# GpSimd as a third issuer for the last tile's stores and loads in a DLRM tower

## The chip, the cores and the metric

The kernel runs on one NeuronCore of a Trainium2 chip. A core has TensorE (matrix products, results in PSUM), VectorE, ScalarE, GpSimd and SyncE (SP), and its transfers run on 16 DMA engines. Transfers are issued by SP, ScalarE or GpSimd, each with a queue of its own. The metric is the device time of one execution in microseconds; a kernel's time is the median of its runs.

## What is computed

2048 samples have 26 indices each and a dense vector of 128 numbers. The 26 table rows (128 numbers each) and the dense vector make 27 vectors per sample. All 351 dot products of two different ones of them, with the dense vector appended, go through three layers (479 to 512 to 256 to 1), all in float32:

```
e = stack([tbl_f[ids[:, f]] for f in range(26)], axis=1)      # 2048 x 26 x 128
T = concatenate([r_dense[:, None, :], e], axis=1)             # 27 vectors a sample
Z = einsum('bnd,bmd->bnm', T, T)
h = concatenate([Z[:, iu0, iu1], r_dense], axis=1)            # pairs n < m, then dense
h = maximum(h @ W_top1 + b_top1, 0.0)
h = maximum(h @ W_top2 + b_top2, 0.0)
y = h @ W_top3
```

## The kernel before

The samples are cut into 16 tiles of 128. Two tiles make a unit; there are 8 units, and `END` is 7, the last. For each tile, GpSimd gathers the rows of 16 tables from DRAM by indirect transfers (L418), 16 to a tile; the rows of the ten small tables are looked up on TensorE as products with one-hot columns (`look`). TensorE turns the gathered rows (`turn`), ScalarE copies what was turned or looked up into `T`, and TensorE makes all dot products of a tile in four blocks (`products`, L773), into `gram_ps`. VectorE copies each block into `gram` (L488, semaphore `gram_free`).

In `gram`, the dot products lie by vector in the partitions. For the first layer they must lie by pair in the partitions and by sample along the row. So they go out to DRAM and come back. Four stores (`dots_store`, j = 0 to 3) take 27 partitions of `gram` each. For a unit (two tiles) they go to `dots`, in pieces of 64 numbers (256 B). Then the loads (`pairs_load`, chunks c = 0, 1, 2 of up to 117 pairs each, and `far_load`, 13 rows that belong to chunk 2) bring them back into `pairs`.

The last unit's two tiles are not stored together but one by one, l = 0 and l = 1, to `dots_last`, in pieces of 32 numbers (128 B): 27 x 27 = 729 pieces to a store, 91 KB. SP does this for l = 0 (L345 to L356). For l = 1 there is nothing left in the loop to work on, and the work is spread over two queues: SP issues the stores j = 0, 1 and later the loads of chunks 0 and 2, ScalarE the stores j = 2, 3 (`last_store`, L644) and later the load of chunk 1 and the far rows (`last_load`, L649 and L650). Each issuer waits for all four stores, which together raise `dots_last_stored[1]` to `STORED`, 64, before it issues a load; every transfer adds 16 when it has landed.

TensorE then does the first layer of tile l = 1 (`last_layer1`, L814): first the dense part for the four groups f of 128 outputs, then chunk by chunk:

```
for c in range(PC):
    for f in range(F1C):
        mm = product(f, c, PC)
        if c == PC - 1:
            mm.then_inc(l1_done, 1)
```

`product` waits for the chunk's semaphore `shuffled_last[1][c]`, 16, or 32 for chunk 2, whose far rows are a second load. After it come ScalarE's activations (L636), the second layer (L836), and VectorE's last sums (L507, L509), whose result SP sends out (L392).

GpSimd has no work after its last gather, that of tile 15. Each engine's instructions run in the order in which they are written; between engines only semaphores set the order.

Of the kernel before, what the change touches and what calls it, by code (L numbers as in the profile page):

```python
# [18 lines left out]
BLOCKS = 4  # L19
# [44 lines left out]
def dlrm_tower(nc, r_dense, ids, tables, W1, b1, W2, b2, W3, out):  # L64
# [6 lines left out]
    TILES = B // P  # L71
# [34 lines left out]
    with ExitStack() as ctx:  # L106
# [6 lines left out]
        def sem(name):  # L113
            return ctx.enter_context(nc.semaphore(name))
# [53 lines left out]
        shuffled = [sem(f"shuffled{i}") for i in range(2)]  # L168
        dots_last_stored = [sem(f"dots_last_stored{l}") for l in range(2)]
        shuffled_last = [[sem(f"shuffled_last{l}_{c}") for c in range(PC)] for l in range(2)]  # L170
        stored = sem("stored")
        ident_zero = sem("ident_zero")
        ident_ready = sem("ident_ready")
# [125 lines left out]
        def _(sp):  # L299
# [45 lines left out]
            def shuffle_last(l, groups, chunks):  # L345

                sp.wait_ge(gram_free, BLOCKS * (2 * END + l + 1))
                for j in groups:
                    sp.dma_start(*dots_store(dots_last[l], j, l * NI, (l + 1) * NI)).then_inc(dots_last_stored[l], 16)
                if l == 0:  # L350
                    sp.wait_ge(l1_done, 2 * (END - 1))
                sp.wait_ge(dots_last_stored[l], STORED)
                for c in chunks:
                    sp.dma_start(*pairs_load(dots_last[l], c, last_pairs(l, c))).then_inc(shuffled_last[l][c], 16)
                if l == 0:
                    sp.dma_start(*far_load(dots_last[l], last_pairs(l, PC - 1))).then_inc(shuffled_last[l][PC - 1], 16)  # L356
# [30 lines left out]
                    load_pair_weights(1)  # L387
                    sp.dma_start(w2[:], W2.rearrange("(c p) f -> p c f", p=P)).then_inc(weights_landed, 16)
            shuffle_last(0, range(NJ), range(PC))
            shuffle_last(1, range(NJ // 2), range(0, PC, 2))  # L390
            sp.wait_ge(y_ready, 2 * UNITS)
            sp.dma_start(out.rearrange("(p t) o -> p (t o)", p=P), y[:]).then_inc(stored, 16)  # L392
            sp.wait_ge(stored, 16)
# [1 line left out]
        @block.gpsimd  # L395
        def _(pool):
            nc.gpsimd.memset(ident[:], 0.0).then_inc(ident_zero, 1)
            pool.wait_ge(ident_zero, 1)
            nc.gpsimd.affine_select(out=ident[:], in_=ident[:], compare_op=ALU.not_equal, fill=1.0, base=0,
                                    pattern=[[-1, P]], channel_multiplier=1).then_inc(ident_ready, 1)  # L400
            nc.gpsimd.iota(minus_row[:], pattern=[[0, 1]], base=0, channel_multiplier=-CH,
                           allow_small_or_imprecise_dtypes=True).then_inc(minus_row_ready, 1)

            def gather(t):
                if t == 0:
                    pool.wait_ge(ids_first_landed, 16)
                if t == 1:
                    pool.wait_ge(ids_landed, 16)
                index = ids_first if t == 0 else ids_all[:, t]
                for r in range(NR):  # L410
                    if t >= 2:
                        pool.wait_ge(turned, NR * (t - 2) + r + 1)
                    if t == 1 and r == 2:
                        pool.wait_ge(ids_rows_stored, 16)
                    for n in rounds[r]:
                        if n == 0:
                            continue
                        pool.indirect_dma_start(  # L418
                            rows[:, t % 2, place[n], :], None, tables[n - 1],
                            bass.IndirectOffsetOnAxis(ap=index[:, n - 1:n].bitcast(U32), axis=0),  # L420
                        ).then_inc(rows_landed[t % 2][r], 16)

            for t in range(TILES):
                gather(t)

        @block.vector
        def _(dve):
# [150 lines left out]
        def _(act):  # L578
# [61 lines left out]
            def last_store(groups):  # L640

                act.wait_ge(gram_free, BLOCKS * TILES)
                for j in groups:
                    act.dma_start(*dots_store(dots_last[1], j, NI, 2 * NI)).then_inc(dots_last_stored[1], 16)  # L644

            def last_load(chunks):
                act.wait_ge(dots_last_stored[1], STORED)
                for c in chunks:
                    act.dma_start(*pairs_load(dots_last[1], c, last_pairs(1, c))).then_inc(shuffled_last[1][c], 16)  # L649
                act.dma_start(*far_load(dots_last[1], last_pairs(1, PC - 1))).then_inc(shuffled_last[1][PC - 1], 16)  # L650
# [62 lines left out]
            turn_out(END, 1, 3)  # L713
            h1_out(END - 1, 1)
            turn_out(END, 1, 4)
            last_store(range(NJ // 2, NJ))
            last_h1_out(0)
            last_load(range(1, PC, 2))
            last_h1_out(1)

        @block.tensor
        def _(pe):
# [84 lines left out]
            def last_layer1(l):  # L807
                def product(f, c, first):
                    if c == PC:
                        rhs, kk = dense[:, END % 2, l * P:(l + 1) * P], P  # L810
                    else:
                        pe.wait_ge(shuffled_last[l][c], 32 if c == PC - 1 else 16)
                        rhs, kk = pairs[:KP, END % 2, c, l * P:(l + 1) * P], KP
                    return pe.matmul(last_l1(l, f), w1[:kk, c, f * P:(f + 1) * P], rhs,  # L814
                                     start=(c == first), stop=(c == PC - 1))
# [127 lines left out]
```

## Time and profile before

| what | value |
|---|---|
| median of 3 runs | 367.7 us (367.35 to 368.36) |
| the profiled execution's own time | 367.51 us |
| its span, from the first to the last instruction | 365.7 us |
| TensorE busy | 343.7 us, 94% |
| VectorE, ScalarE, GpSimd busy | 223.3, 172.5, 255.7 us |
| mean granted TensorE clock | 0.985 of full speed |

The span is measured on one profiled execution; 1.8 us of its time lie outside it. A TensorE busy for 94% leaves little waiting, and a share over the whole span says nothing on a single place: the rows below are those of the places that the change touches. Times in rows count from the span's start.

### The profile page before, as it was taken

To read this page: it belongs to the slowest core of one execution; us is meant where nothing else is said; L and a number is where in the kernel's file an instruction comes from. 1 tells how busy PE (TensorE), PEld (TensorE's weight loads), DVE (VectorE), ACT (ScalarE), POOL (GpSimd) and SP (SyncE) were. 2 spreads that over 40 slices of the span, in tenths; PEclk is the share of its full clock that TensorE was granted. 3 is DMA by queue.
4 is the path that set the end of the run, shared out by engine and by line. 5 is a ranking of instruction groups with operands and counts; after the bars stand their busy time and mean duration, and the time that the engine had idled before them with its cause. 6 is when DMAs were issued, how large, how long until landed. Compare 5 with 4: busy or idle time off the path is not lost.

```text
span 365.7 us, 9897 instructions
## 1 busy us (share of the span) xinstructions
PE 343.7 (94%) x4042; PEld 321.2 (88%) x4042; DVE 223.3 (61%) x786; ACT 172.5 (47%) x220; POOL 255.7 (70%) x263
## 2 busy tenths in 40 slices
PE   3997898879899999999999999999999999999976
PEld 1887798869889999999989998999999998998866
DVE  3989969976826485556927394656828493622311
ACT  4266737553456244553466153643476154435111
POOL 6788877777777777777777777777777777775000
PEclk9999999989999999999999999999999999999986
DMA  7996232353525522354225522462225321544030
GB/s 206 262 257 189 66 124 62 92 144 109 179 59 135 170 58 52 87 130 147 58 52 138 167 60 50 103 182 79 60 52 136 96 60 52 120 112 86 21 61 1
DMA packets 45878, 39.07 MB, mean 107 GB/s; under 512 B 32930, under 2 KB 39113, under 8 KB 45834
## 3 DMA queue, kind: packets, MB, share of 16 engines
q1 hardware_dynamic: 36014, 21.40, 22.1%
q0 software_dynamic: 8192, 16.79, 17.4%
q8 instruction: 32, 0.52, 0.6%
q10 hardware_dynamic: 1628, 0.25, 0.5%
q14 instruction: 12, 0.10, 0.1%
HBM read 32.40 MB, written 6.02 MB: 105 GB/s over the span
## 4 chain that ended last, share of the span: by engine, by line
PE 82%; DMA 6%; ACT 6%; DVE 3%; issue 2%; ACTq 0%; SPq 0%; DVEq 0%
PE look_ps L747 35%; PE gram_ps L773 15%; PE mlp_ps L793 13%; PE look_ps L757 7%; PE mlp_ps L803 7%; DMA ids_near<-ids_rows 2%; ACT T L614 2%; PE look_ps L738 2%; DVE hot L464 2%; DMA ids_rows<-rows 1%; DMA dots_last<-gram 1%; ACT T L606 1%; ACT tab_hi L582 1%; PE mlp_ps L814 1%; DMA ids_all<-in_ids_dram 1%
## 5 line engine op out<-in xcount | busy, mean ns | idle before, releaser
L418 POOL DMA_INDIRECT rows<-in_tbl_dram,ids_all x240 | 236.9, 987 | 73.2 <-issue 71.3
L464 DVE TENSOR_SCALAR hot<-ids_near 125x256 fp32r<-125x256 f16 x640 | 149.1, 304 | 41.9 <-PE look_ps L747 35.4
L747 PE MATMUL look_ps<-hot,tab_hi 125*128 125x256 f32 x616 | 154.4, 290 | 6.4 <-DVE tab_lo L447 2.2
L747 PE MATMUL look_ps<-hot,tab_lo 125*128 125x256 f32 x616 | 150.2, 283 | 0.0
L747 PEld LDWEIGHTS look_ps<-hot,tab_hi 125*128 125x128 f32 x616 | 117.8, 191 | 8.2 <-issue 3.8
L747 PEld LDWEIGHTS look_ps<-hot,tab_lo 125*128 125x128 f32 x616 | 118.1, 192 | 0.1
L614 ACT COPY T<-look_ps 128x384 f32<-128x384 f32 (+1 forms) x80 | 85.3, 1109 | 69.1 <-PE look_ps L757 69.0
L488 DVE COPY gram<-gram_ps 128x432 f32<-128x432 f32 x64 | 38.8, 607 | 68.6 <-PE gram_ps L773 66.5
L606 ACT COPY T<-look_ps 128x512 f32<-128x512 f32 x32 | 38.7, 1208 | 74.2 <-PE look_ps L747 69.0
L773 PEld LDWEIGHTS gram_ps<-T 128*54 128x54 f32 x2048 | 54.5, 131 | 8.2 <-issue 4.5
L773 PE MATMUL gram_ps<-T 128*54 128x54 f32 x2048 | 57.8, 215 | 1.9 <-DVE gram L488 1.2
L757 PE MATMUL look_ps<-ident,rows 128*128 128x128 f32 x272 | 41.8, 277 | 1.2 <-issue 1.2
L793 PE MATMUL mlp_ps<-pairs,w 117*128 117x256 f32 x168 | 40.9, 379 | 0.0
L757 PEld LDWEIGHTS look_ps<-ident,rows 128*128 128x128 f32 x272 | 31.3, 142 | 3.3 <-issue 1.4
L793 PEld LDWEIGHTS mlp_ps<-pairs,w 117*128 117x128 f32 x168 | 30.7, 189 | 3.7
L803 PE MATMUL mlp_ps<-w,h 128*128 128x256 f32 x112 | 25.4, 380 | 0.9 <-ACT h L629 0.9
L803 PEld LDWEIGHTS mlp_ps<-w,h 128*128 128x128 f32 x112 | 20.7, 190 | 3.7 <-ACT h L629 1.1
L629 ACT ACTIVATE h<-mlp_ps,bias 128x128 f32<-128x128 f32 x56 | 16.1, 383 | 12.9 <-PE mlp_ps L793 12.9
L418 POOL DMA_INDIRECT rows<-in_tbl_dram,ids_first x16 | 18.0, 1124 | 5.7 <-issue 4.6
L591 ACT ACTIVATE ids_near<-ids_near,minus_row 125x2560 f16<-125x2560 f16 x7 | 17.1, 2441 | 0.7 <-DMA ids_near<-ids_rows 0.7
L793 PE MATMUL mlp_ps<-dense,w 128*128 128x256 f32 x56 | 16.7, 379 | 0.0
L602 ACT COPY T<-look_ps 128x256 f32<-128x256 f32 x16 | 11.3, 706 | 6.4 <-PE look_ps L747 6.0
(72 smaller groups left out, 137.3 us busy)
## 6 DMA issues: line engine op xcount, KB each, us to landing
dots<-gram SPq DMA_DIRECT2D x28, 182.2 KB
ids_near<-ids_rows SPq DMA_DIRECT2D x7, 640.0 KB, 6.2
rows<-in_tbl_dram,ids_all POOLq DMA_INDIRECT x240, 2.6
T<-in_tbl_dram SPq DMA_DIRECT2D x5, 448.0 KB
pairs<-dots SPq DMA_DIRECT2D x14, 117.0 KB
rows<-in_r_dense_dram SPq DMA_DIRECT2D x16, 64.0 KB
gram<-in_tbl_dram SPq DMA_DIRECT2D x2, 448.0 KB
pairs<-dots SPq DMA_DIRECT2D x7, 104.0 KB
```

What stands on the lines that cost most here:

```text
L418: pool.indirect_dma_start(rows[:, t % 2, place[n], :], None, tables[n - 1], bass.IndirectOffsetOnAxis(ap=index[:, n - 1:n].bitcast(U32), a ...
L464: eq = nc.vector.tensor_scalar(hot[:VP, at % 2, c], ids_near[:VP, u % 2, k], float(c), None, ALU.is_equal)
L488: nc.vector.tensor_copy(gram[:, :, :, first:first + PER], gram_ps[:, b % 2, 0:2 * PER * NV].rearrange("p (i s n) -> p s n i", s=2, n=NV)). ...
L591: nc.scalar.activation(ids_near[:VP, u % 2], ids_near[:VP, u % 2], ACT.Identity, bias=minus_row[:VP]).then_inc(ids_relative, K)
L606: nc.scalar.copy(T_unit(u)[:, :, :, n0:n1 + 1:n1 - n0].rearrange("p l q n -> p n l q"), src.rearrange("p (n l q) -> p n l q", n=2, l=2)).t ...
L614: nc.scalar.copy(T_tile(u, l)[:, :, n:n + cnt].rearrange("p q n -> p n q"), look_ps[:, bank_of(("turn", u, l, r)), 0:cnt * P].rearrange("p ...
L629: relu = nc.scalar.activation(by_sample[:, g], by_pair[:, g], ACT.Relu, bias=bias1[:, f:f + 1])
L747: mm = pe.matmul(dst, w[:VP, k, c], hot[:VP, slot, c], start=(c == 0 and half == 0), stop=(c == CH - 1 and half == 1))
L757: mm = pe.transpose(look_ps[:, bank, i * P:(i + 1) * P], rows[:, l, place[n], :], ident[:])
L773: mm = pe.matmul(gram_ps[64 * g:64 * g + 2 * NV, b % 2, at:at + 2 * NV], src[:, g, i], src[:, g, i], start=True, stop=True)
L793: mm = pe.matmul(mlp_ps[:, f * 2 // F1C, f % 2], w1[:kk, c, f * P:(f + 1) * P], rhs, start=(c == 0), stop=(c == PC))
L803: mm = pe.matmul(mlp_ps[:, 0, l], h1[:, c, l * P:(l + 1) * P], w2[:, c], start=(c == 0), stop=(c == F1C - 1))
```

## The change

For the last tile, l = 1, GpSimd becomes a third issuer. It sends store j = 3, which ScalarE sent, once the last copy is done, and loads chunk 2, which SP loaded. It gets two semaphores, `pool_stored` for its store and `pool_loaded` for its load. SP keeps stores 0, 1 and chunk 0; ScalarE keeps store 2, chunk 1 and the far rows. All three wait for `pool_stored` at 16 and `dots_last_stored[1]` at 48 before they load. TensorE waits, before chunk 2, for `pool_loaded` and for the far rows. Nothing else is changed; the transfers are the same eight, in the same sizes.

```diff
+        pool_stored = sem("pool_stored")
+        pool_loaded = sem("pool_loaded")
...
                 if l == 0:
                     sp.wait_ge(l1_done, 2 * (END - 1))
-                sp.wait_ge(dots_last_stored[l], STORED)
+                if l == 0:
+                    sp.wait_ge(dots_last_stored[l], STORED)
+                else:
+                    sp.wait_ge(pool_stored, 16)
+                    sp.wait_ge(dots_last_stored[l], STORED - 16)
...
             shuffle_last(0, range(NJ), range(PC))
-            shuffle_last(1, range(NJ // 2), range(0, PC, 2))
+            shuffle_last(1, range(NJ // 2), range(1))
...
             for t in range(TILES):
                 gather(t)
+
+            pool.wait_ge(gram_free, BLOCKS * TILES)
+            pool.dma_start(*dots_store(dots_last[1], NJ - 1, NI, 2 * NI)).then_inc(pool_stored, 16)
+            pool.wait_ge(pool_stored, 16)
+            pool.wait_ge(dots_last_stored[1], STORED - 16)
+            pool.dma_start(*pairs_load(dots_last[1], PC - 1, last_pairs(1, PC - 1))).then_inc(pool_loaded, 16)
...
             def last_load(chunks):
-                act.wait_ge(dots_last_stored[1], STORED)
+                act.wait_ge(pool_stored, 16)
+                act.wait_ge(dots_last_stored[1], STORED - 16)
...
-            last_store(range(NJ // 2, NJ))
+            last_store(range(NJ // 2, NJ - 1))
             last_h1_out(0)
-            last_load(range(1, PC, 2))
+            last_load(range(1, PC - 1))
             last_h1_out(1)
...
-                        pe.wait_ge(shuffled_last[l][c], 32 if c == PC - 1 else 16)
+                        if l == 1 and c == PC - 1:
+                            pe.wait_ge(pool_loaded, 16)
+                        pe.wait_ge(shuffled_last[l][c], 32 if l == 0 and c == PC - 1 else 16)
```

The end of SP's queue before, from the far rows of tile l = 0 on; a row is a line of the kernel, the transfer, what it writes and reads, its shape and its waits:

```order
L356 DMA pairs<-dots_last 13x128
L349 DMA dots_last<-gram 729x1x32 [waits gram_free]
L349 DMA dots_last<-gram 729x1x32
L354 DMA pairs<-dots_last 117x1x128 [waits dots_last_stored1]
L354 DMA pairs<-dots_last 104x1x128
L392 DMA out_dram<-y 128x16 [waits y_ready]
```

And now (lines of the changed kernel are counted anew):

```order
L362 DMA pairs<-dots_last 13x128
L351 DMA dots_last<-gram 729x1x32 [waits gram_free]
L351 DMA dots_last<-gram 729x1x32
L360 DMA pairs<-dots_last 117x1x128 [waits dots_last_stored1,pool_stored]
L398 DMA out_dram<-y 128x16 [waits y_ready]
```

The load of 104 rows, chunk 2, has left the queue, and the load of chunk 0 waits for one more semaphore.

The end of ScalarE's queue before, with the activations of both tiles' first layer (L636) around its loads:

```order
L644 DMA dots_last<-gram 729x1x32 [waits gram_free]
L644 DMA dots_last<-gram 729x1x32
L636 ACTIVATE h<-look_ps,bias 128x2x2x32 [waits l1_done]
L636 ACTIVATE h<-look_ps,bias 128x2x2x32
L636 ACTIVATE h<-look_ps,bias 128x2x2x32 [waits l1_done]
L636 ACTIVATE h<-look_ps,bias 128x2x2x32
L649 DMA pairs<-dots_last 117x1x128 [waits dots_last_stored1]
L650 DMA pairs<-dots_last 13x128
```

And now:

```order
L656 DMA dots_last<-gram 729x1x32 [waits gram_free]
L648 ACTIVATE h<-look_ps,bias 128x2x2x32 [waits l1_done]
L648 ACTIVATE h<-look_ps,bias 128x2x2x32
L648 ACTIVATE h<-look_ps,bias 128x2x2x32 [waits l1_done]
L648 ACTIVATE h<-look_ps,bias 128x2x2x32
L662 DMA pairs<-dots_last 117x1x128 [waits dots_last_stored1,pool_stored]
L663 DMA pairs<-dots_last 13x128
```

One store is gone from ahead of the activations. It stands now at the end of GpSimd's queue, behind the gathers of tile 15, with the load of chunk 2 behind it:

```order
L424 DMA rows<-in_tbl_dram,ids_all 128x128 [waits turned]
L424 DMA rows<-in_tbl_dram,ids_all 128x128
L433 DMA dots_last<-gram 729x1x32 [waits gram_free]
L436 DMA pairs<-dots_last 104x1x128 [waits dots_last_stored1,pool_stored]
L106 UNCONDITIONAL_BRANCH
```

Before, the branch that ends the queue followed the gathers.

## Rows read from the trace of the kernel before

**Rows 1.** The page: shares of the engines in the chain that ended last.

```profile
PE 82%; DMA 6%; ACT 6%; DVE 3%; issue 2%; ACTq 0%; SPq 0%; DVEq 0%
```

**Rows 2.** The chain of work, last 20 us: start us, us, what.

```profile
346.11 0.62 DVE gram L488
...
346.75 1.62 ACTq L644
...
348.41 4.11 DMA dots_last<-gram
352.51 0.02 issue
352.53 2.51 DMA pairs<-dots_last
...
355.08 1.22 PE mlp_ps L814 x4
...
358.87 0.85 PE mlp_ps L814 x4
```

**Rows 3.** Timeline, 346 to 354, ScalarE and SP: start us, us, engine, line.

```profile
346.74 1.58 SPq L349 DMA_DIRECT2D dots_last<-gram  x2
...
346.75 2.44 ACTq L644 DMA_DIRECT2D dots_last<-gram  x2
349.23 1.27 ACT L636 ACTIVATE h<-look_ps,bias 128x128 f32<-128x128 f32 x4 [9.61 <-issue]
```

**Rows 4.** Windows of 0.25 us (last two columns: DMA share, GB/s); packets, 347 to 352.4.

```profile
348.00:348.25 0.25, 0.25 (x5) 0.25 (x4) 0.23 (x2) 0.00 (x0) 0.00 (x0) 1.00 0.14 27
...
349.25:349.50 0.25, 0.25 (x5) 0.25 (x4) 0.00 (x0) 0.25 (x2) 0.00 (x0) 1.00 0.77 122
...
351.25:351.50 0.25, 0.25 (x3) 0.20 (x3) 0.00 (x0) 0.00 (x0) 0.00 (x0) 1.00 0.91 96
351.50:351.75 0.25, 0.25 (x4) 0.25 (x3) 0.06 (x1) 0.00 (x0) 0.00 (x0) 1.00 0.50 51
...
DMA packets 2952, 0.37 MB, mean 69 GB/s; under 512 B 2952, under 2 KB 2952, under 8 KB 2952
```

**Rows 5.** DMA view, 314.3 to 321.9, a unit's stores: share in 40 slices, queues.

```profile
DMA  0746566677437478976656987683697766349300
...
q1 hardware_dynamic: 2952, 0.75, 44.4%
```

**Rows 6.** TensorE's last dense products; windows with its clock (third from last); L814 alone.

```profile
351.94 0.61 PE L814 MATMUL gram_ps<-dense,w 128*128 128x128 f32 x4
...
354.50:354.75 0.25, 0.00 (x0) 0.00 (x0) 0.00 (x0) 0.00 (x0) 0.00 (x0) 0.69 0.52 156
354.75:361.25 6.50, 6.17 (x27) 5.99 (x28) 0.00 (x0) 1.50 (x4) 0.00 (x0) 0.50 0.05 14
...
346.20:349.60 3.40, 3.40 (x32) 3.40 (x31) 1.00 0.30 50
355.40:360.50 5.10, 5.10 (x24) 4.88 (x23) 0.50 0.01 2
```

**Rows 7.** GpSimd's gathers: timeline, windows and the page's list of issues.

```profile
329.38 0.94 POOL L418 DMA_INDIRECT rows<-in_tbl_dram,ids_all  x1 [0.30 <-issue]
...
334.39 0.95 POOL L418 DMA_INDIRECT rows<-in_tbl_dram,ids_all  x1 [0.30 <-issue]
...
330.25:331.00 0.75, 0.75 (x5) 0.67 (x4) 0.72 (x2) 0.75 (x1) 0.44 (x2) 1.00 0.00 0
331.00:331.25 0.25, 0.25 (x3) 0.22 (x2) 0.25 (x3) 0.15 (x1) 0.25 (x1) 1.00 0.84 197
...
rows<-in_tbl_dram,ids_all POOLq DMA_INDIRECT x240, 2.6
```

**Rows 8.** Another fall of the clock: timeline of TensorE, windows.

```profile
76.66 0.36 PE L747 MATMUL look_ps<-hot,tab_hi 125*128 125x256 f32 x1 [2.17 <-DVE tab_lo L447]
...
78.25:81.25 3.00, 2.84 (x34) 2.47 (x35) 2.06 (x10) 1.57 (x2) 2.36 (x3) 0.50 0.33 88
```

## The prediction

> **What bounds the kernel now.** I read the page's own list of the costliest chain first: TensorE carries it nearly to the end, so what matters is where TensorE stands still [rows 1]. Then I read the chain of work over the last 20 us in order of time [rows 2]. It shows one hole. The last copy of the products ends at 346.11 + 0.62 = 346.73. From there the chain is ScalarE's queue issuing (1.62 us), a store in flight (4.11 us), a load in flight (2.51 us), and only at 355.08 does TensorE go on; from 355.08 to the end it is TensorE, then VectorE, then the output. The change touches the stretch from 346.73 to 355.08, and nothing ahead of it.
>
> In that stretch both queues start at once, SP at 346.74 and ScalarE at 346.75, and each issues two stores [rows 3]. The windows by DMA share show the first data at about 348.2, some 100 to 120 GB/s until 351.50, and a window about half full after that [rows 4]. So the four stores divide into 1.45 us before any data, 351.63 - 348.2 = 3.4 us of data, and 352.51 - 351.63 = 0.88 us from the last data to the release of the loads (351.63 is where I put the end in the half-full row 351.50:351.75). The data do not wait for the issues: the last issue begins at 348.41 [rows 2] and ends at 346.75 + 2.44 = 349.19 [rows 3], over two microseconds before the last data.
>
> What holds the data back? The packets of the stretch are 2952, which is 4 x 738, and a store has 729 pieces of 128 B [rows 4]; 738 is 729 + 9, so I read nine engines per store with one closing packet each. Four stores one tile earlier in the loop, with pieces of 256 B, are 2952 packets too, but those spread over some 6.8 us instead of 3.4, 36 of the 40 slices of 0.19 us [rows 5], with gathers beside them. Twice the bytes, twice the time: the limit lies in the DMA engines that carry the pieces, and not in issuing. One store is worth 3.4 / 4 = 0.85 us of that.
>
> **The change, part by part.**
>
> *ScalarE's second store goes.* ScalarE is free at 346.75 + 1.62 = 348.37 instead of 349.19, 0.82 us earlier; its activations began at 349.23, right behind the issue [rows 3]. They make TensorE's following products ready sooner by a few tenths. Worth nothing at the end, since after those and the dense products TensorE stands idle from 352.55 for 2.5 us anyway [rows 2, 6]. The three hardware stores, alone, would have their last data at 351.63 - 0.85 = 350.78 and be landed at 350.78 + 0.88 = 351.66. That is the most that this part gives: 0.85 us.
>
> *GpSimd's store comes in.* GpSimd's last gather starts at 334.39 and takes 0.95 us [rows 7], so the engine has been idle for 11 us when the copies end and can start at about 346.8. Its issue is the unknown price, call it G. The trace has no plain GpSimd transfer, only gathers of 128 rows of 512 B. From below, G is what a gather takes, 0.95 us, if the number of pieces costs nothing. From above, all of the 0.95 us is work per row: 7.4 ns a piece, times 729, 5.4 us. I take the middle, 3.2 us, because some of a gather's time must be fixed and nothing in the rows says how much. After the issue a gather's data show 0.68 us later (issue 329.38 + 0.94 = 330.32, data in the window from 331.00, and none in the one before) [rows 7]. Then the store's own data, at most 0.85 us, and 0.88 us to land. Sum: 346.8 + G + 0.68 + 0.85 + 0.88 = 349.21 + G. With G = 0.95 that is 350.2, below the hardware stores' 351.66, so those decide and the gain is 0.85. With G = 3.2 it is 352.4, next to no gain. With G = 5.4 it is 354.6, a loss of 2.1 us. Data that start before the issue ends, or more engines than nine, would pull the middle down by some tenths; for these I take about half of the 0.85, so the middle lands at 352.0.
>
> *Shared engines.* If the GpSimd store sits on the same nine engines as the others, the 2952 packets stay on them and only an earlier start could help. By the Trainium skill (DMA: Bandwidth & Descriptors, Why a DMA increments its semaphore by 16 and not by 1), a transfer runs on the largest count up to 16 that divides the outer size of both sides, for hardware queues the lowest engines; the trace agrees, with 9 closing packets for 27 partitions against 729 rows. For GpSimd it names consecutive engines from a moving start; no row here shows which.
>
> *The waits.* SP, ScalarE and GpSimd wait for two semaphores where they waited for one; both are full before they go, or the later decides. Queued behind that wait on SP is the load of chunk 0, for which TensorE waits at 355.08; on ScalarE it is chunk 1 and, behind it, the last layer's activations, which are not due before the last chunk's products, from 358.87 on [rows 2].
>
> *Chunk 2 goes from SP to GpSimd.* TensorE takes the chunks in turn: the stretch of the chain from 355.08 to 358.87 covers chunks 0 and 1 [rows 2]. So chunk 2 is wanted 3.8 us after chunk 0, even at twice the clock 1.9 us after. A gather of slightly more data needs 2.6 us from issue to landing [rows 7], chunk 0 needs 2.51: chunk 2 lands about when chunk 0 does. Nothing, with 3 us of cover. SP's queue loses an issue that nobody waited for.
>
> *The clock.* TensorE's granted clock falls from full to half (2.4 to 1.2 GHz) at about 354.6, two microseconds into its idle time (from 351.94 + 0.61 = 352.55), and is still half until 361.25 [rows 6]. So nearly all of the last layer runs at half clock. The same kind of products takes 5.1 us for 24 there and 3.4 us for 32 at full clock [rows 6], 212 ns against 106 each. I keep that state in the sum.
>
> **The sum.** Landing of the stores, 352.51, becomes about 352.0, and all that follows moves by 0.5: 367.51 (the profiled execution's own time) - 0.5 = 367.0. The median of the runs shown is 0.2 above that execution, so 367.2.
>
> **The rivals.**
>
> *No gain, because the engines were the limit.* The third queue brings the same 738 packets to the same engines; landing stays at 352.5 and the time at 367.7. For it: the level rate across the seam between the queues, and the 256 B stores. Against it: whatever of the load goes to the seven others. The Trainium skill has this as a rule (DMA: Bandwidth & Descriptors, Issuing engines are not separate DMA queues): transfers from several issuers interleave on the same 16 engines, and more issuers only save issue time. By it the gain is nil here.
>
> *Slower, because GpSimd writes the pieces one by one.* Place: GpSimd's issue of the store, between 346.8 and the loads. It decides from G = 3.3 us on, 4.5 ns a piece, and is over the measurement's 1.1 us (0.3%) from G = 4.4. At the gather's full 7.4 ns a piece the time is 367.7 + 2.1 = 369.8. For it: this transfer has nearly six times as many pieces as a gather. Against it: a gather must look up an index for each row, a plain store needn't. A gentler case, G from 3.3 to 4.4, is no change.
>
> *Clearly faster, because the clock holds.* If TensorE waits 1.7 us instead of 2.5, it goes on at 354.2, ahead of the 354.6 where the clock fell. If the clock then stays full, the 6.5 us at half clock [rows 6] become some 3.2 us: 367.7 - 0.8 - 3.2 = 363.7. For it: the fall comes late in the idle time. Against it: at 78 us the clock falls while TensorE is busy, over a microsecond after a shorter idle stretch of 2.17 us [rows 8]; a fall is not ended by work that has just begun.
>
> **How the numbers follow.** A measurement of this kernel can tell about 1.1 us (0.3%). Small gain, 0.2 to 0.8 us: 0.40. No gain through shared engines or G of 3 to 4.4: 0.24. Slower through G above 4.4: 0.26. Clock holds: 0.10. The first two are "same" but for a little at the edges: faster 0.13, same 0.60, slower 0.27. The range goes up to 369.8, the price of 7.4 ns a piece, and down to 366.3, which is the full 0.85 us and the runs' own scatter of 0.6; only the clock's case and a dearer GpSimd than the bound lie outside.
>
> **What would show it.** GpSimd's queue has a transfer on the products at about 346.8, and its length is G. Right: the loads are released between 351.7 and 352.4, by a hardware store, and TensorE goes on 2.5 us later. Wrong towards slower: GpSimd's issue runs past 350, SP's loads wait for it, and the data share falls to nothing before the GpSimd packets come. Shared engines: the data end at 351.5 again. The clock's case: no half clock in the last ten microseconds. Chunk 2 would be wrong if TensorE had a wait between its second and third chunk.

## The result and the profile after

The changed kernel takes 369.37 us (median of 22 runs) against 366.28 us for the kernel before (22 runs); the ratio of the times is 1.008, 95% interval 1.0059 to 1.0101, some 3 us slower by the medians. One of the changed kernel's 22 runs took 560.11 us at a mean clock of 0.566; it is left out of the ratio. The profiled execution took 369.87 us, its span is 368.1 us, its mean granted clock 0.985.

The chain of work of the changed kernel, its last 20 us (start us, us, what), answers to [rows 2]:

```profile
347.66 0.62 DVE gram L500
...
349.13 5.84 DMA dots_last<-gram
...
355.03 2.45 DMA pairs<-dots_last
...
357.52 1.22 PE mlp_ps L829 x4
358.74 0.85 PE gram_ps L829 x4
...
366.12 0.06 DVEq L106
```

Times here must be counted from the end of the last copy, 347.66 + 0.62 = 348.28. From there to the loads, 355.03, it is 6.75 us; before it was 352.53 - 346.73 = 5.80 us. I call this the **stretch**, and it grew by 0.95. The store that ends it comes from SP's queue, a hardware one, and is 5.84 us in flight; before, the one at the chain's end was 4.11. Behind the stretch nothing changed: load 2.45 us, and from TensorE's first chunk to the last row's end 366.18 - 357.52 = 8.66 us at half clock. The rest of the difference between the two spans, 348.28 - 346.73 = 1.55 us, stands ahead of the copies, where nothing was changed; I come back to it.

The timeline of the changed kernel, 346 to 358, answers to [rows 3] (in brackets: us that the engine sat idle before, and what ended it):

```profile
348.30 1.60 SPq L351 DMA_DIRECT2D dots_last<-gram  x2
348.30 1.62 ACTq L656 DMA_DIRECT2D dots_last<-gram  x1
...
348.57 1.01 POOL L433 DMA_DIRECT2D dots_last<-gram  x1 [12.15 <-DVE gram L500]
...
349.97 0.64 ACT L648 ACTIVATE h<-look_ps,bias 128x128 f32<-128x128 f32 x2 [8.79 <-PE look_ps L829]
...
355.58 0.63 POOL L436 DMA_DIRECT2D pairs<-dots_last  x1 [6.00 <-DMA dots_last<-gram]
...
357.52 0.80 PE L829 MATMUL mlp_ps<-pairs,w 117*128 117x128 f32 x2 [3.52 <-DMA pairs<-dots_last]
```

GpSimd's issue of 729 pieces took 1.01 us, no longer than a gather of 128 rows [rows 7]. It was done at 349.58. ScalarE's only store took it 1.62 us, as the first of two did before, and SP's two took 1.60 together. So all issues were over by 349.92, five microseconds before the release, and issuing isn't what made it late. TensorE's wait went from 2.5 to 3.52 us, and it had no other wait between chunks.

The DMA view of the changed kernel, 347 to 356 (the last number of an issue is us to landing; a queue's last number is the time of its packets as a share of the 16 engines' time):

```profile
DMA packets 2279, 0.39 MB, mean 44 GB/s; under 512 B 2251, under 2 KB 2251, under 8 KB 2278
...
q1 hardware_dynamic: 1476, 0.19, 13.7%
q0 software_dynamic: 64, 0.10, 9.8%
q10 hardware_dynamic: 738, 0.09, 7.0%
...
dots_last<-gram POOLq DMA_DIRECT2D x1, 91.1 KB, 5.1
```

And the same view of the kernel before, 345 to 354:

```profile
q10 hardware_dynamic: 1476, 0.19, 16.1%
q1 hardware_dynamic: 1476, 0.19, 13.7%
```

A store that the hardware queues send is 738 packets. GpSimd's is 64 at most, 27 of them between 2 and 8 KB (2278 - 2251): its 729 pieces travel some 27 to a packet. Its packets took 9.8% of the engines' time, ScalarE's store of the same bytes 7.0% here and 16.1 / 2 = 8.05% before. But the three queues add up to 13.7 + 9.8 + 7.0 = 30.5%, and the two of before to 29.8%, so the packets' time hardly grew; and it isn't a measure of the engines' work, since a window below shows a share of 1.15, which only packets that overlap in time can give. And GpSimd's store landed at 348.57 + 5.1 = 353.7, 1.3 us before the loads were released. It was neither the last nor the quick one.

Windows of 0.25 us of the changed kernel (last two columns: DMA share, GB/s), with the clock third from last; they answer to [rows 4] and [rows 6]:

```profile
350.50:350.75 0.25, 0.25 (x4) 0.25 (x4) 0.00 (x0) 0.11 (x1) 0.00 (x0) 1.00 1.15 113
...
351.25:351.50 0.25, 0.25 (x4) 0.22 (x3) 0.00 (x0) 0.08 (x1) 0.00 (x0) 1.00 0.56 37
...
353.50:353.75 0.25, 0.25 (x5) 0.25 (x3) 0.21 (x2) 0.00 (x0) 0.00 (x0) 1.00 0.43 52
353.75:354.00 0.25, 0.25 (x3) 0.06 (x1) 0.25 (x2) 0.00 (x0) 0.00 (x0) 1.00 0.13 17
...
357.00:363.50 6.50, 5.98 (x26) 5.89 (x27) 0.00 (x0) 1.50 (x4) 0.00 (x0) 0.50 0.06 19
```

Data went until about 353.9, 5.6 us after the copies; before it was 351.63 - 346.73 = 4.9 us, and they ended within one window. The level rate of before is gone: in the midst of the data it falls to 37 GB/s for a window, and at the end it thins out from 353.5 on, over half a microsecond. Half a microsecond in the midst of it by queue, 351.0 to 351.5, 2.7 us after the copies:

```profile
q0 software_dynamic: 15, 0.02, 56.2%
q10 hardware_dynamic: 42, 0.01, 6.5%
q1 hardware_dynamic: 20, 0.00, 3.2%
```

and of the kernel before at the same distance, 349.5 to 350.0:

```profile
q10 hardware_dynamic: 358, 0.04, 57.7%
q1 hardware_dynamic: 124, 0.02, 20.1%
```

The two hardware queues moved 62 packets where they moved 482. While GpSimd's packets are under way the hardware stores nearly stand still: by half microseconds from 350.0 they move 308, 233, 62, 170 and 323 packets. The profiles of e1, e5, e12, e16 and e18 have the same gap, with 48 to 66 packets in the half microsecond at that distance.

The clock is at half (1.2 GHz) from 357.00 to beyond 363.50, about as long as in the profile of before.

### The profile page after: what moved, and what is told of

It reads as the page before. It is cut to its first block, busy times and chain, and to the rows that moved or that the text cites. A ratio compares the mean times of both kernels' runs of the same rounds, so it can differ in the third digit from the quotient of the medians.

```text
span 368.1 us, 9904 instructions
## 1 busy us (share of the span) xinstructions
PE 343.4 (93%) x4042; PEld 320.9 (87%) x4042; DVE 222.9 (61%) x786; ACT 172.3 (47%) x220; POOL 258.3 (70%) x265
## 4 chain that ended last, share of the span: by engine, by line
PE 81%; DMA 6%; ACT 6%; DVE 3%; issue 2%; SPq 0%; DVEq 0%; ACTq 0%
PE look_ps L760 35%; PE gram_ps L786 15%; PE mlp_ps L806 13%; PE look_ps L770 7%; PE mlp_ps L816 7%; DMA ids_rows<-rows 2%; ACT T L626 2%; DMA dots_last<-gram 2%; PE look_ps L751 1%; DVE hot L476 1%; DMA ids_near<-ids_rows 1%; ACT T L618 1%; ACT tab_hi L594 1%; PE mlp_ps L829 1%; DMA ids_all<-in_ids_dram 1%
## 5 line engine op out<-in xcount | busy, mean ns | idle before, releaser
L641 ACT ACTIVATE h<-mlp_ps,bias 128x128 f32<-128x128 f32 x56 | 16.1, 383 | 12.9 <-PE mlp_ps L806 12.9
```

The source lines that it names most:

```text
L641: relu = nc.scalar.activation(by_sample[:, g], by_pair[:, g], ACT.Relu, bias=bias1[:, f:f + 1])
```

## The experiments

Experiments e1 to e11 ran on chips on which every kernel, the one before too, took 505 to 540 us, with TensorE standing still in the loop (busy for 75 to 77% of the span in e1 to e4 and e8, against 94%). Their whole times decide nothing: e2 and e8, whose stretch is that of before and for which a ratio within 0.002 of 1 was expected, have 0.9951 and 0.9935, while e3 and e4, with the stretch longer and shorter, both have 1.0049. Only durations of the last stretch are read from them. e12 to e18 ran on chips where the kernel before takes 366 to 367.5 us.

**Store alone (e1, e16) and load alone (e2, e15).** One half of the change each:

```diff
-            shuffle_last(1, range(NJ // 2), range(1))
+            shuffle_last(1, range(NJ // 2), range(0, PC, 2))
...
-            pool.dma_start(*pairs_load(dots_last[1], PC - 1, last_pairs(1, PC - 1))).then_inc(pool_loaded, 16)
```

(e1, against the changed kernel; e2 has the load and leaves all four stores as before.)

> Only the store goes to GpSimd, chunk 2 stays with SP. In the profile of the changed kernel the stretch from the last copy to the release of the loads is 6.69 us against 5.78 before. Theory A (GpSimd's pieces hold up the hardware stores' data): the stretch stays at 6.5 to 6.9 us here, and the whole time is as far above the kernel before as the changed kernel, ratio 1.006 to 1.010. Rival B (the load on GpSimd costs something, at the end or elsewhere): the ratio falls to 1.002 or less although the stretch is long, and the rest of the loss belongs to the load.

> Only the load of chunk 2 goes to GpSimd; both stores stay with ScalarE. Theory A: the stretch from the last copy to the release of the loads is 5.8 us as before, the load lands under the products of chunks 0 and 1, ratio 1.000 within 0.002. Rival B: ratio 1.003 or more, with TensorE waiting ahead of its third chunk or losing time elsewhere.

> Only the store j = 3 is GpSimd's. Late theory: stretch 6.5 to 7 us, and the changed kernel's whole loss, 2 to 3 us, ratio 1.005 to 1.009. Early theory: the same loss or less, with the hole at 93 us over 2 us.

> Only the load of chunk 2 is GpSimd's; the four stores stay with SP and ScalarE. Late theory (the loss is the longer stretch of the stores and the clock that falls in it): as before, ratio 0.998 to 1.002, stretch 5.8 us. Early theory (something that any addition to GpSimd's queue brings, seen as TensorE's hole at 93 us, 2.35 to 3.6 us long in three profiles with the change and 0.8 to 1.2 us in two without): hole over 2 us, and the time 1 to 2 us above before, ratio 1.003 to 1.005.

The chain of the store alone, e1:

```profile
507.71 0.62 DVE gram L496
...
509.18 5.62 DMA dots_last<-gram
...
514.86 2.44 DMA pairs<-dots_last
```

and of the load alone, e15:

```profile
347.34 0.62 DVE gram L492
...
349.64 4.11 DMA dots_last<-gram
...
353.77 2.68 DMA pairs<-dots_last
...
356.49 0.71 PE mlp_ps L820 x4
```

Store alone: stretch 514.86 - 508.33 = 6.53 us, and 6.52 in e16, whose time is 368.07 us, ratio 1.0047 (1.0012 to 1.0081). Load alone: stretch 353.77 - 347.96 = 5.81 us, as before; 367.02 us, ratio 1.0017 (0.9981 to 1.0052). The store alone lengthens the stretch, and the load's effect can't be told from nothing.

**Two stores for GpSimd (e3).** GpSimd sends j = 2 and 3, ScalarE none.

```diff
-            pool.dma_start(*dots_store(dots_last[1], NJ - 1, NI, 2 * NI)).then_inc(pool_stored, 16)
+            for j in range(NJ // 2, NJ):
+                pool.dma_start(*dots_store(dots_last[1], j, NI, 2 * NI)).then_inc(pool_stored, 16)
```

> GpSimd sends both of ScalarE's stores, ScalarE none; the suspected cost is doubled. Theory A: the stretch from the last copy to the release grows by about another 0.9 us, to 7.4 to 7.8 us, and the ratio to the kernel before rises to 1.010 or more. Rival C (one GpSimd store is only unlucky in its place, its data take no more of the engines than a hardware store's): the stretch stays at 6.7 us or falls, since GpSimd's issue of about 1 us each ends by 350.5.

```profile
509.45 0.62 DVE gram L501
...
510.36 0.95 POOL dots_last L434
511.31 5.00 DMA dots_last<-gram
...
516.32 3.03 DMA pairs<-dots_last
```

The chain (last copy, GpSimd's second issue, a store, a load) shows a stretch of 516.32 - 510.07 = 6.25 us. One theory expected 7.4 to 7.8 us. But e3 is not the changed kernel with a store added: a hardware store has gone as well. By e4, next, two hardware stores alone would need 4.85 - 0.95 = 3.9 us (an estimate), so both GpSimd stores together cost some 2.35 us, where one costs 1.9. SP's stores lost about as much time as with one: 1472 of their 1476 packets went from about 511.5 to 515.0, 3.5 us where e4's pace gives 1.6. The chain ends not with them but with GpSimd's own second store. So the delay isn't a price per GpSimd store that adds up.

**Three stores (e4).** GpSimd sends no store; a fourth of the last tile's dot products is replaced by the other tile's, stored earlier by SP, so that only three transfers run in the stretch.

```diff
+            sp.dma_start(*dots_store(dots_last[1], NJ - 1, 0, NI)).then_inc(pool_stored, 16)
...
-            pool.dma_start(*dots_store(dots_last[1], NJ - 1, NI, 2 * NI)).then_inc(pool_stored, 16)
```

> As the changed kernel, but GpSimd sends no store: the part of the intermediate tensor that it would fill is filled ahead of time, from the other tile's columns, by a fifth store of SP behind the four of tile l = 0, so a quarter of the last tile's dot products is the other tile's. Three hardware stores are left after the last copy. Theory A: without GpSimd's pieces the three need 4.9 to 5.1 us from the last copy to the release (5.78 less one store's 0.85), as the prediction had it, so the changed kernel's 6.69 is all GpSimd's doing. Rival C (three stores on two queues need as long as four, the start or the landing being the limit): 5.7 us or more. In the whole, A without other losses: 0.997 to 0.999; if some of the loss does not lie in the stores, 1.000 or more.

```profile
508.29 0.62 DVE gram L500
...
509.74 3.96 DMA dots_last<-gram
...
513.76 2.54 DMA pairs<-dots_last
```

The chain gives a stretch of 513.76 - 508.91 = 4.85 us, 0.95 less than before. Its hardware queues move 412, 429, 479 and 476 packets in the half microseconds from 510.5, with no gap. With three stores in hardware queues the prediction's 4.93 was right. GpSimd's store, added to these three, costs 6.75 - 4.85 = 1.9 us; a fourth hardware store costs 0.95. At e4's pace, 1796 packets in 2 us, the 1096 packets of the changed kernel's 2.5 us from 350.0 would take 1.2 us, so by this estimate 1.3 of the 1.9 us are lost in the gap.

**Who issues the hardware stores (e8).** SP sends three, ScalarE one, GpSimd nothing.

```diff
-            shuffle_last(1, range(NJ // 2), range(0, PC, 2))
+            shuffle_last(1, range(NJ - 1), range(0, PC, 2))
...
-            last_store(range(NJ // 2, NJ))
+            last_store(range(NJ - 1, NJ))
```

> The kernel before, with three stores on SP and one on ScalarE instead of two and two. If the DMA engines that carry the pieces are the limit, as the prediction took it, the stretch from the last copy to the release stays at 5.7 to 5.9 us and the ratio at 1.000 within 0.002. If issuing were the limit, SP's third issue would end at 2.4 us instead of 2.45 and nothing would change either, but with ScalarE's first issue of 1.6 us as the limit the stretch would shorten by up to 0.8 us.

```profile
498.06 4.21 DMA dots_last<-gram
...
502.28 2.49 DMA pairs<-dots_last
```

Stretch 502.28 - 496.42 = 5.86 us, against 5.80. So it makes no difference which of the two queues issues the hardware stores. That the engines hold them, as the prediction had it, fits this, and e4, where a store fewer takes 0.95 us off.

**A GpSimd transfer with long pieces (e11).** As e4, and GpSimd sends, instead of its store, 91 KB of other data in 128 pieces of 728 B.

```diff
+            pool.dma_start(scratch, rows[:, 0].rearrange("p n d -> p (n d)")[:, 0:182]).then_inc(pool_stored, 16)
```

> As the run with three hardware stores (a fifth store of SP behind tile l = 0 fills the missing quarter from the other tile's columns, so a quarter of the last tile's dot products is the other tile's), but GpSimd issues at its place a transfer of 93 KB that nothing reads, in 128 pieces of 728 B instead of 729 of 128 B, and everyone waits for it. The stretch from the last copy to the issue of the loads was 4.85 us with no GpSimd transfer and 6.5 to 7.0 with its store. Theory F (many small pieces in GpSimd's packets hold the shared engines): 4.8 to 5.3 us here. Rival G (any third transfer of 91 KB, or GpSimd's queue as such, holds the hardware stores up): 6 us or more.

The chain around the stretch:

```profile
494.29 0.62 DVE gram L506
...
500.19 2.50 DMA pairs<-dots_last
```

GpSimd's issue in the timeline:

```profile
495.20 0.59 POOL L438 DMA_DIRECT2D scratch<-rows  x1 [47.34 <-DVE gram L506]
```

a window of its data, which came before those of the hardware stores, and its transfer in the list of issues (last number us to landing):

```profile
496.25:496.50 0.25, 0.25 (x4) 0.25 (x4) 0.16 (x2) 0.00 (x0) 0.00 (x0) 1.00 1.02 262
...
scratch<-rows POOLq DMA_DIRECT2D x1, 91.0 KB, 2.5
```

Stretch 500.19 - 494.91 = 5.28 us: 0.43 above e4. The same bytes from the same engine cost the hardware stores 0.43 us in 128 pieces and 1.9 us in 729. The transfer landed 2.5 us after its issue instead of 5.1. But more differs than the size of the pieces. In the window shown only GpSimd's queue moved data, 0.07 of its 0.09 MB; the hardware stores' data came after it, at 92 to 121 GB/s until 499.25, about what they have alone in e4. So most of GpSimd's data went ahead of the others' and not among them. It also moves other data to another place, and its outer size is 128 and not 27, over engines that I don't know. So this shows that a GpSimd transfer beside the stores needn't cost them 1.9 us; it supports the many small pieces as the cause and doesn't prove it. The issue took 0.59 us against 1.01; if the pieces make the difference, that is (1.01 - 0.59) / 601 = 0.7 ns a piece, an estimate.

**The changed kernel again (e5, e12, e18).** No edit.

> The changed kernel once more, unedited, with the granted clock of every run of both kernels. In one profile each, the stretch from the last copy to the release of the loads explains 0.9 us of a loss of about 2.9. Theory D (the longer wait, 3.5 us against 2.5, makes TensorE's clock fall more often): the kernel before shows a larger part of its runs at a mean clock of 0.99 or more than the changed kernel, and the ratio is again 1.006 to 1.010. Rival E (something early in the program is slower, for instance the gathers): both kernels show the same clocks and the changed one has a last copy 1 to 2 us later in every profile.

> The changed kernel, unedited, a third time, for a chip on which the loop is undisturbed: there the whole-time loss (1.008) can be set beside the clocks of every run of both kernels. Theory D (beside the 0.9 us of the stretch, the longer wait lets TensorE's clock fall in runs in which it held before): the runs of the kernel before fall into two groups about 3 us apart, the lower one with about 6.8 us less at half clock, and the changed kernel has fewer runs in the lower group. Rival E: no such groups, both kernels' runs spread alike around medians 2 to 3 us apart.

> One look at the changed kernel, for the same hole. Early theory: over 2.3 us again. Late theory: 0.8 to 3.6 us; the stretch is 6.5 to 7 us.

Stretches 501.50 - 494.50 = 7.00, 357.82 - 351.12 = 6.70 and 353.16 - 346.43 = 6.73 us. With the first profile, and e10 and e14 below, all runs in which GpSimd sends one of the four stores lie from 6.5 to 7.0 us, and all with hardware stores at 5.80 to 5.86. e12's time was 369.83 us against 366.68, ratio 1.0045 (1.0002 to 1.0087), in which its two longest runs don't count. Its clocks are used below.

**The hole at 93 us (e17, e18).** Ahead of the copies the first profile had been 1.55 us late, and its chain showed TensorE's wait for gathered rows 2.80 us long there, against 1.24 before. e12 had 3.59 and e14 2.35, e13 without the change 0.77. So a share of the loss could be from there. One profile more of either kernel:

> One look at the kernel before, for the hole at 93 us. Early theory: 0.8 to 1.3 us again. Late theory: anything that a gather's variation gives, 0.8 to 3.6 us.

The last copy of e17, without the change:

```profile
347.40 0.62 DVE gram L488
```

The chain of the changed kernel in e18, the hole, and the last copy:

```profile
93.35 0.82 issue
...
345.81 0.62 DVE gram L500
```

Here the hole is 0.82 us with the change, and the last copy ends at 346.43, ahead of e17's 347.40 + 0.62 = 348.02 without it (e17 has no such wait at all). e15 and e16 have 0.99 and 1.84 us. So a kernel with GpSimd's store can go without the long hole. But four of five such profiles have 1.84 us or more, and none of the four without that store has over 1.24, so the profiles alone don't clear the hole. In e12 and e16 the clock fell at its end too, at 95 and 97 us. What speaks against a large share is e14, below: it has the store and a hole of 2.35 us, and over twelve runs the kernel loses only 0.35 to 0.5 us against e13. That leaves little room for 1.55 us there.

**The wait filled (e6, e7, e9, e10, e13, e14).** Dummy products of 128x128, whose results nobody reads, in TensorE's wait for the first chunk, to see whether the clock then stays at full. e6 and e7 had 22 and 31, which was too many (4.91 and 6.92 us, longer than the wait); then 11 for the kernel before (e9, e13), 15 for the changed one (e10, e14).

```diff
+                for _ in range(11):
+                    pe.matmul(look_ps[:, 0, 0:P], ident[:], ident[:], start=True, stop=True)
                 for c in range(PC):
```

> The kernel before, with 22 extra products of 128 columns (the identity by itself, into a PSUM bank that is no longer needed) where TensorE waits for the last tile's chunks: 2.3 us of its 2.5 us wait. Theory D: the clock stays at full in the last layer, which then takes about 3.3 us less where it fell before; since it does not fall in every run, ratio 0.992 to 0.997 and less scatter. Rival (the clock falls anyway, or its fall costs nothing that the median shows): ratio 0.999 to 1.001.

> The changed kernel, with 31 such extra products, 3.3 us of its 3.5 us wait. Theory D: without the clock only the longer stretch is left of the loss, so this kernel is 0.9 us (0.25%) above the other one with extra products, and the stretch is 6.5 to 6.9 us as before. Rival E (an early loss): it is 2 to 3 us above it.

> The kernel before with 11 extra products where TensorE waits for the last tile's chunks, 2.45 us of the 2.5 us wait (the 22 of the earlier run took 4.91 us, so they reached past the wait by 2.4 us and gave back most of what the clock won). Theory D: the last layer runs at full clock and the time from the release of the loads to the end falls from 8.6 us to about 6.0; in the whole, ratio 0.992 to 0.997 where the rest of the program is steady. Rival (the fall is not caused by the wait): the last layer still shows half clock, ratio 1.000.

> The changed kernel with 15 extra products, 3.35 us of its 3.5 us wait. Theory D: from the release of the loads to the end about 6.0 us here too, and the stretch from the last copy to the loads' issue still 6.5 to 7.0 us, so the time is 0.7 to 1.2 us above the run of the kernel before with its wait filled. Rival E (a loss elsewhere in the program): 2 us or more above it.

> The kernel before with 11 dummy products of 128x128 in TensorE's wait for the last tile's first chunk; nothing else differs, and the output is the same. Clock theory (a wait of 2.5 us that lets the granted clock fall for the last layer is worth some 3 us, and a longer wait makes the fall come in more runs): the last layer runs at full clock in every run, first chunk to end 5.6 to 5.8 us instead of 8.6, and the whole time is 1.5 to 3 us below before, ratio 0.992 to 0.996. Its rival (the clock's fall costs nothing in the whole time, the loss is only a longer stretch of stores): ratio 0.999 to 1.001.

> The changed kernel with 15 such products in its longer wait. Clock theory: the last layer at full clock in every run, so what stays of the loss is the longer stretch alone, 0.7 to 1.2 us above the filled kernel of before; against the plain kernel before it is 0.5 to 2 us faster. Rival (the stretch is the whole loss, or something early in the program is): it stays 2 to 3 us above before, as the changed kernel does.

The chain of e13, the kernel before with 11 products, from its dummies on:

```profile
353.30 2.46 PE look_ps L828 x22
355.76 0.70 PE mlp_ps L814 x4
356.46 0.45 PE gram_ps L814 x4
...
361.42 0.06 DVEq L106
```

and of e14, the changed kernel with 15:

```profile
353.76 3.35 PE look_ps L843 x30
357.11 0.55 PE mlp_ps L829 x4
...
362.62 0.06 DVEq L106
```

Four products take 0.45 us where they took 0.85 after the unfilled wait, and from the first chunk to the end it is 361.48 - 355.76 = 5.7 us in place of 8.6 (5.66 in e9, 5.68 in e10). So the fall costs 3 us when it lasts through the layer, the 3.2 of the prediction's clock rival. It doesn't always. In the profiles with an unfilled wait and the stretch of before, the first chunk to the end takes 8.70 us (before), 8.63 (e2), 7.36 (e17), 7.20 (e8) and 5.73 (e15); with GpSimd's one store it takes 8.66, 8.63 (e1), 8.52 (e5), 8.33 (e18), 7.31 (e12) and 7.30 (e16); in e4, whose stretch is the shortest, 5.74. The means of the first two groups are 7.5 and 8.1. In time: e13 366.2 us against 367.46 of the kernel before, ratio 0.9963 (0.9939 to 0.9987); e14 366.66 us, ratio 0.9996 (0.9961 to 1.0031). With the wait filled the change costs 0.5 us by the medians and 0.35 by the means, where it cost 2 to 3. So most of the loss went through the clock in the last layer. Expected of e13 were 1.5 to 3 us of gain with a full clock in every run; it was 1.3 by the medians, because many runs of the kernel before end at full clock anyway. e15 is such a run: its chain above goes on with 0.45 us for four products.

**The clocks of all runs.** Each run comes with its mean granted clock c and its span s. The clock has two levels, so a run was at half for 2(1 - c)s, and lost half of that where TensorE had work. The mean does not say where it fell: e15 has 0.991 by two falls near 39 and 80 us, and none in its last layer. Over the runs of e12 to e18's chips, and the 22 of the changed kernel's result (one of 560.11 us, and one of 1171.62 us of the kernel before, left out; so are e17 and e18, of one run each):

| kernel | runs | with c of 0.994 or more | mean at half clock | mean time |
|---|---|---|---|---|
| before | 62 | 26 | 5.4 us | 366.8 us |
| changed | 33 | 5 | 7.7 us | 369.0 us |
| store alone (e16) | 12 | 2 | 7.0 us | 368.6 us |
| load alone (e15) | 12 | 4 | 6.0 us | 367.0 us |
| before, filled (e13) | 12 | 10 | 3.6 us | 366.3 us |
| changed, filled (e14) | 12 | 11 | 2.8 us | 366.6 us |

The growth of the stretch plus half of the growth at half clock should give the growth of the mean. Changed: 0.95 + (7.7 - 5.4) / 2 = 2.1, measured 369.0 - 366.8 = 2.2. For the other rows I use the kernel before of the same chip. Store alone: 0.72 + (7.0 - 5.0) / 2 = 1.7, measured 2.2. Before, filled: (3.6 - 5.6) / 2 = -1.0, measured -0.9. Changed, filled: 0.7 + (2.8 - 5.6) / 2 = -0.7, measured -0.6; the 0.7 is how much later than before its first chunk came after the last dot products, (357.11 - 347.37) - (355.08 - 346.08). Load alone: (6.0 - 5.0) / 2 = 0.5, measured 0.5; with the same stretch as before this is the scatter of twelve runs. The sums leave no more than 0.5 us over in any row. Another cut of the same runs agrees in the main: at a mean clock of 0.991 the changed kernel's 15 runs take 369.4 us and the 27 of before 367.8, at 0.986 nine take 369.6 and four 368.6. At the same clock it is 1.0 to 1.6 us slower, which is the stretch and up to 0.65 us that stays open.

## Why the prediction was wrong

It said 367.2 us with no change that can be told as the likeliest, and the change is 2 to 3 us slower. The value lies in the range by luck: the upper end was the price of a slow issue, which didn't come, and it was counted from 367.7 us, the median of three runs, where 22 runs of the kernel before have 366.28. Counted from there, the same 2.1 us end at 368.4.

*What bounds the kernel* was right in its place, the stretch between the last copy and the loads, and nearly in its price, 0.85 us a store (0.95 in e4); the split of the issues doesn't matter (e8). The argument from the stores of 256 B was not sound. It set a queue alone with gathers beside it against two queues without. In the same profile SP's four stores of tile l = 0, also alone and with gathers, but in pieces of 128 B, move their 2952 packets from about 331.5 to 335.9, 4.4 us, and those of 256 B theirs from about 314.9 to 321.2, 6.3 us (37 of the 40 slices show data, not 36, gathers included). Twice the bytes took 1.4 times as long, so much of the price is one per piece. Nor does a row show nine engines: it was read from the 9 packets over 729, and the share of the 16 engines goes up to 0.92, where nine would be 0.56. Packets that overlap in time may explain that.

*G* was taken at 3.2 us and is 1.01, the lower bound of 0.95. That alone would have put the prediction further off: with it, the prediction says that the three hardware stores decide and the gain is the full 0.85.

*The step that failed* is the one on shared engines: "the 2952 packets stay on them and only an earlier start could help", and with it the sum's 351.66 for the hardware stores as something that GpSimd's store can't move. It can. The hardware stores were released 6.75 us after the copies, in place of 4.93 with no store beside them (4.85 in e4), or 5.80 with a fourth of their own kind, and the packets by queue show where: 62 in half a microsecond in place of 482, while GpSimd's run. My floor for sharing was "no gain", and it should have had a price below it. The prediction had put the cost of a GpSimd store to the stores beside it at nothing; it is 1.9 us (6.75 - 4.85). The packets don't stay 2952: 738 small ones became 64, 27 of them of 2 KB and more.

By the Trainium skill (DMA: Bandwidth & Descriptors, Queues, rings and completion order), a DMA engine goes round between the queues and changes only at the end of a packet. By the same page of the Trainium skill (SWDGE vs HWDGE vs iDMA) a GpSimd packet is preferably at most 4096 B, and at most 64 descriptors. The trace agrees on the size: 91.1 KB in 27 packets and some small ones is at most 3.4 KB each. That a hardware piece then waits behind some 27 pieces of 128 B is argued and not shown: it fits e1 and e11, but not easily e3, where twice as many such packets cost little more. The rule of the Trainium skill (DMA: Bandwidth & Descriptors, Issuing engines are not separate DMA queues) that more issuers only save issue time gave "no gain" as the worst. Here the stretch grew by 0.7 to 1.2 us.

*The slow rival* had the right sign and the wrong place. It looked for the loss in GpSimd's issue, from G = 3.3 us on. GpSimd issued quickly, its own store landed 1.3 us early, and other queues' stores were late.

*ScalarE's freed issue* was worth nothing, as said. Its activations began 349.97 - 348.28 = 1.7 us after the copies in place of 2.5, and TensorE stands idle later anyway.

*Chunk 2* was free, as said: 2.3 us from issue to landing, no wait of TensorE before it, and no time that could be told in e15.

*The clock* I kept at half for the last layer ("I keep that state in the sum"), from one profile. That was a second error of size: the state isn't the kernel's but the run's. 26 of 62 runs of the kernel before have a mean clock of 0.994 or more, at most 4.4 us at half, of which [rows 8] has 3.00 at 78 us; so they ended without the long fall. Of the changed kernel's runs 5 of 33 have such a mean. Both are lower bounds, since a lower mean can come from falls elsewhere, as in e15. A stretch that grows by 0.95 us went with a loss of over 2. That filling the wait takes most of this back is shown (e13, e14). That it is the length of the wait, and nothing else in the changed kernel, that makes the fall more frequent is what the store alone and the filled kernels point to; it wasn't tried by lengthening the wait of the kernel before.

Open are why the hardware queues nearly stand still while GpSimd's packets run, why two GpSimd stores cost them little more than one, and on which engines GpSimd's pieces run; no view here tells. No run changed the number of pieces alone, so the pieces as the cause stay likely and unproven.

## What to carry to other kernels

A further issuer is free only if its transfer is free for those beside it. Before moving one of several concurrent transfers of small pieces to GpSimd, ask what it does to the hardware queues' transfers in the same microseconds, and price the mix below "no gain". When TensorE waits a few microseconds near the end, read the clock over many runs and not one, since a fall in some of them can turn 1 us of wait into 2; some harmless products in the wait took 1.3 us off the kernel before, more than the 0.85 us that this change could have taken off the stores.

## What the runs showed of the hardware

GpSimd issues a plain transfer of 729 pieces in 1.01 us and one of 128 pieces in 0.59 us, an estimated 0.7 ns a piece; its gathers of 128 rows take 0.95 and more. ScalarE's one store of the stretch takes it 1.62 us and its later loads 0.78 and 0.82, and in e3, where it sent no store, its first load took 1.57 us. So the first transfer of ScalarE's program was the dear one, a store or a load.
